# Attention with shifted queries: the sum of queries and maxima moved from a PSUM bank to GpSimd

## Chip, cores and metric

One core of one Trainium2 chip. The metric is the device time of one execution in microseconds (us); lower is better. The kernel was executed three times for timing and once more with the hardware profiler.

## What is computed

A hidden state of 16 x 256 tokens with 128 features goes through a transformer layer with experts, then through a retention block, then through the same layer again. The attention of such a layer, for one batch element and head, is this:

```
xn = layer_norm(x)                       # 256 tokens x 128
q, k, v = xn @ Wq + bq, xn @ Wk + bk, xn @ Wv + bv
for each of 16 heads (8 features each):
    s = q_h @ k_h.T / sqrt(8)            # 256 x 256
    p = exp(s - max(s, keys))            # the shift cancels below
    out_h = (p @ v_h) / sum(p, keys)
x1 = layer_norm(x + out @ Wo + bo) * g1 + b1
```

Behind it each token goes to one of four expert networks by a router, and a second layer norm follows.

## The kernel before

The layer runs as two phases (`phase(0)` and `phase(BATCH)`), each over 16 batch elements, with the retention block between them and the experts' tiles at the end of each. Elements are numbered 0 to 15 in the first phase and 16 to 31 in the second. The engines are driven by five instruction streams written out by hand; each engine works its stream strictly in order and waits on semaphores. For every element `i` a function `body(i)` per engine holds the work of iteration `i`, and this work is software-pipelined: iteration `i` also does parts of elements `i + 2` (layer norm before attention, "prep"), `i + 1` (projection), `i - 1` (the rest of its heads), `i - 2` (output projection, layer norm "ln1", x1), `i - 3` (router positions) and `i - 4` (sorted rows written to memory, `sort_out`).

An iteration has eight slots, p = 0 to 7. In slot p, TensorE issues a burst (`score_burst`): the raw scores of heads 2p and 2p + 1 of element i (L591), interleaved with the shifted, transposed scores (L597) of two heads that are five slots behind. VectorE takes the negated maximum over the raw scores (`maximum`, L1374), which lie in one pair of PSUM banks (`score_duo`); ScalarE takes the exponential of the shifted scores (`exp`, L1064) from another pair (`prob_duo`). Neither pair is doubled, so the next burst waits for both.

Heads are handled in four groups g of four. The stacked queries `q_st` and keys `k_st` of a group are made by `expand` (L584, L585) on TensorE and `out_expand` (L1050) on ScalarE. Once all the maxima of group g are there, they have to be added to the queries: in the stack, each head has spare rows beside its 8 feature rows, and one of them carries the shift, so that the product of stacks gives score minus maximum. This is `spread_max`, L629 and L631: TensorE first copies the queries `q_st[:, g]` through an identity into a spare bank (256 columns), then adds the transposed maxima from `mx` (two matmuls of 128 columns). ScalarE's `shift_q` (L1056) copies the sum to `q2_st[:, g]` in SBUF, rounded to fp32r, and signals `q2_ready`. It runs in slot 3 for g = 0, slot 5 for g = 1, slot 7 for g = 2 and slot 1 of the next iteration for g = 3. Its reader, the L597 part of the burst, comes two slots later each time: slots 5, 7, and 1 and 3 of the next iteration. The spare bank `a` (or `c`) is taken by `take`, which waits for the last reader of the bank; in slot 2 `expand` for g = 2 takes bank `a` after `shift_q` for g = 3 of the element before.

GpSimd's stream in iteration i is: place the first half of the values (`place_v(i, 0)`, L1867), the two indirect DMAs of `sort_out(i - 4)` (L1907), the layer norm "prep" for i + 2 (`rstd`, L1842 to L1846, `normalise`, L1854), `add_bo` (L1859), the layer norm "ln1" for i - 2 (L1842 to L1846, L1854), `make_x1` (L1872, L1874), `route_product` (L1880), `own_row` (L1892), and the second half of the values (`place_v(i, 1)`, L1867). The values come from one buffer `v_nat`, which ScalarE fills (`out_v`, L1043) in slot 1: it waits until both halves of the element before have been placed (`vb_ready`). In slot 1 ScalarE's order is `exp`, `out_v`, `out_pv` (L1072), `shift_q` for g = 3; all its later work stands behind them.

The calls in GpSimd's `body(i)` that the change goes between are

```
if live(i, base):
    place_v(i, 0)
...
    add_bo(i + 2, base)
...
    normalise(i - 2, "ln1", lambda t: y1[:, t, :], lambda t: n1[:, t, :], i - 1 - base // BATCH)
    make_x1(i - 2, base)
```

## Time and profile before

| | us |
|---|---|
| median of three timed runs | 901.46 (901.03 to 902.38) |
| profiled execution, its own time | 902.45 |
| its span in the trace | 900.6 |
| TensorE matmul / weight load busy | 812.1 / 609.2 |
| VectorE busy | 740.8 |
| ScalarE busy | 650.5 |
| GpSimd busy | 549.7 |

The profiled execution took 902.45 us, 1.85 us more than its span, which begins with the first instruction shown and ends with the last. Engines are named PE (TensorE matmuls), PEld (TensorE weight loads), DVE (VectorE), ACT (ScalarE), POOL (GpSimd) and SP (SyncE). Busy times overlap. A line such as L1374 is a line of the kernel. Ends of matmuls are modelled, and they are pipelined, so matmuls that stand in a row overlap in the trace. In a timeline, `[0.21 <-POOL v_st L1867]` means that the engine idled 0.21 us before the instruction and that the one named released it; a line with xN merges N instructions, and starts of neighbours on one engine can overlap by the pipeline of the engine.

### The profile page before, as it was taken

What the parts mean: (1) busy time and instruction counts of PE and PEld (TensorE: products, weight loads), DVE (VectorE), ACT (ScalarE), POOL (GpSimd) and SP (SyncE); (2) the same over time, 40 slices, a digit from 0 to 9 for tenths busy, and PEclk for the clock granted to TensorE, in tenths of its full rate; (3) what the DMA queues carried; (4) which work ended last, traced back from release to release, by engine and by line L of the source; (5) the groups of instructions that cost most, each with busy time, mean ns of one, the idle gap of its engine ahead of it and who ended that gap; (6) DMA issues with size and microseconds to landing.
All of it is one profiled execution on the core that took longest, in us unless ns stands there. A gap on an engine that the chain in (4) does not pass through costs nothing.

```text
span 900.6 us, 26130 instructions
## 1 busy us (share of the span) xinstructions
PE 812.1 (90%) x8479; PEld 609.2 (68%) x8479; DVE 740.8 (82%) x1841; ACT 650.5 (72%) x1242; POOL 549.7 (61%) x914
## 2 busy tenths in 40 slices
PE   4989999999999699399999988999999999987894
PEld 3656666666665699367878766666666666656894
DVE  4688999999996788569898875789998989967895
ACT  2578888888886488335454554888989889873794
POOL 4126667676755667628676772157676766556676
PEclk9999999999999999789999996999999999999997
DMA  9995699100004688210000000000000000045781
GB/s 281 378 419 143 126 401 415 70 12 24 12 18 145 194 235 275 74 46 2 0 0 0 1 1 1 2 2 14 24 12 23 12 18 18 14 150 171 235 276 49
DMA packets 41813, 96.65 MB, mean 107 GB/s; under 512 B 5224, under 2 KB 25470, under 8 KB 37260
## 3 DMA queue, kind: packets, MB, share of 16 engines
q1 hardware_dynamic: 36236, 83.11, 28.3%
q0 software_dynamic: 5504, 12.63, 3.9%
q8 instruction: 37, 0.61, 0.3%
q14 instruction: 36, 0.29, 0.1%
HBM read 43.64 MB, written 53.13 MB: 107 GB/s over the span
## 4 chain that ended last, share of the span: by engine, by line
PE 57%; DVE 16%; POOL 11%; issue 11%; ACT 2%; DMA 2%; DVEq 0%; SPq 0%; POOLq 0%; ACTq 0%
PE duo L648 10%; PE duo L591 10%; DVE mx L1374 6%; PE duo L584 4%; PE duo L740 3%; PE duo L900 2%; PE duo L585 2%; PE duo L629 2%; PE duo L879 2%; PE duo L567 2%; PE duo L888 2%; PE duo L858 2%; POOL out L1964 2%; PE duo L861 2%; PE duo L631 2%
## 5 line engine op out<-in xcount | busy, mean ns | idle before, releaser
L1374 DVE TENSOR_REDUCE mx<-duo 128x4 fp32r<-128x1024 f32 x256 | 313.5, 1225 | 64.5 <-PE duo L591 57.5
L1064 ACT ACTIVATE probs<-duo 128x1024 f32<-128x1024 f32 x256 | 262.8, 1027 | 42.1 <-PE duo L597 33.8
L591 PE MATMUL duo<-stacks 32*128 32x256 f32 x1024 | 133.4, 339 | 24.7 <-DVE mx L1374 19.9
L648 PE MATMUL duo<-probs,v_st 128*32 128x256 f32 x2048 | 143.1, 399 | 0.5
L597 PE MATMUL duo<-q_st,stacks 32*128 32x256 f32 x1024 | 131.6, 335 | 0.1
L591 PEld LDWEIGHTS duo<-stacks 32*128 32x128 f32 x1024 | 80.3, 191 | 69.0 <-DVE mx L1374 27.0
L1050 ACT ACTIVATE stacks<-duo,small 128x512 fp32r<-128x512 f32 x128 | 88.8, 694 | 9.0 <-PE duo L585 8.4
L584 PE MATMUL duo<-qk_hi,sel_r 128*128 128x256 f32 x256 | 82.5, 342 | 4.1 <-DVE qk_lo L1363 3.5
L648 PEld LDWEIGHTS duo<-probs,v_st 128*32 128x32 f32 x2048 | 54.8, 112 | 42.8 <-issue 4.8
L740 PE MATMUL duo<-w,xs 128*128 x608 | 78.1, 283 | 5.9 <-DVE hidden L1542 2.8
L740 PEld LDWEIGHTS duo<-w,xs 128*128 128x128 f32 x608 | 73.8, 198 | 7.9 <-issue 7.7
L597 PEld LDWEIGHTS duo<-q_st,stacks 32*128 32x128 f32 x1024 | 78.2, 188 | 1.4 <-ACT probs L1064 0.5
L1907 POOL DMA_INDIRECT x_sorted<-rows,pos_all x64 | 66.9, 1045 | 13.0 <-issue 13.0
L1056 ACT ACTIVATE q_st<-duo 128x256 fp32r<-128x256 f32 x128 | 49.4, 386 | 34.5 <-PE duo L631 33.4
L585 PE MATMUL duo<-qk_lo,sel_r 128*128 128x256 f32 x256 | 69.2, 291 | 0.0
L1842 POOL TENSOR_TENSOR a_prep<-mv_prep,eps_ln 128x2 f32<-128x2 f32 x32 | 6.0, 189 | 102.2 <-DVE mv_prep L1339 102.2
L1094 ACT ACTIVATE xs<-duo,wside 128x256 f32<-128x256 f32 x152 | 59.2, 470 | 9.1 <-PE duo L726 8.8
L584 PEld LDWEIGHTS duo<-qk_hi,sel_r 128*128 128x128 f32 x256 | 50.4, 197 | 21.0 <-ACT q_st L1056 5.1
L1867 POOL TENSOR_TENSOR v_st<-v_nat,ones_wide 128x128 f32<-128x128 f32 x64 | 29.6, 462 | 49.1 <-ACT v_nat L1043 28.9
L1679 DVE TENSOR_TENSOR ret<-duo,dm 128x768 f32<-128x768 f32 x64 | 58.0, 947 | 1.2 <-PE duo L882 1.2
L629 PE MATMUL duo<-stacks,ident_r 128*128 128x256 f32 x128 | 53.0, 414 | 0.0
L629 PEld LDWEIGHTS duo<-stacks,ident_r 128*128 128x128 f32 x128 | 24.6, 193 | 41.6 <-issue 36.9
(222 smaller groups left out, 2057.7 us busy)
## 6 DMA issues: line engine op xcount, KB each, us to landing
x_sorted<-ret SPq DMA_DIRECT2D x2, 17476.0 KB, 52.7
wbuf<-w_pack SPq DMA_DIRECT2D x38, 512.0 KB
ret<-x_sorted SPq DMA_DIRECT2D x22, 257.0 KB, 3.1
stacks<-x_sorted SPq DMA_DIRECT2D x12, 257.0 KB, 3.9
wside<-w_pack SPq DMA_DIRECT2D x38, 66.0 KB
w_pack<-wbuf SPq DMA_DIRECT2D x2, 1024.0 KB, 8.4
decay_rows<-prow SPq DMA_DIRECT2D x1, 1536.0 KB
xs<-x_sorted SPq DMA_DIRECT2D x4, 257.0 KB, 3.6
```

Source lines behind the costliest of these rows:

```text
L584: pe.matmul(half, sel_r[:, g, 2 * n, :], qk_hi[:, n, :], start=True, stop=False)
L585: last = pe.matmul(half, sel_r[:, g, 2 * n + 1, :], qk_lo[:, n, :], start=False, stop=True)
L591: return pe.matmul(score_bank[h % 2][:, t * SEQ:(t + 1) * SEQ], q_st[r:r + 32, g, t * P:(t + 1) * P], k_st[r:r + 32, g, :], start=True, st ...
L597: return pe.matmul(banks[h % 2][:, t * SEQ:(t + 1) * SEQ], k_st[r:r + 32, g, t * P:(t + 1) * P], q2_st[r:r + 32, g, :], start=True, stop=True)
L629: pe.matmul(o[:, 0:SEQ], ident_r[:], q_st[:, g, :], start=True, stop=True)
L648: last = pe.matmul(into[32 * j:32 * j + 32, :], v_st[:, half, t, first:first + VC], probs[:, (g * GH + j) % RING, t, :], start=(t == 0 and ...
L740: last = pe.matmul(sum_bank(k)[:, t * P:(t + 1) * P], hid[:, n % 2, c, t * P:(t + 1) * P], w2[:, bass.ds(e * CPE + c, 1), :], start=(c == ...
L1050: act.activation(both_st[:, :, g, :], o.rearrange("p (n t) -> p n t", n=2), ACT.Identity, bias=ones_col[:]).then_inc(ex_ready, 1)
L1064: act.activation(probs[:, h % RING:h % RING + 2, :, :], duo_now[:].rearrange("p (n t q) -> p n t q", n=2, t=TT), ACT.Exp, scale=SCALE).the ...
L1094: act.activation(hid[:, n % 2, c, :], bank[c][:, 0:SEQ], ACT.Relu, bias=wside[:, n % 3, c:c + 1]).then_inc(h_ready, 1)
L1374: dve.tensor_reduce(rows, score_duo[:].rearrange("p (n t k) -> p n t k", n=2, t=TT), AX.X, ALU.max, negate=True).then_inc(max_done, 1)
L1907: pool.indirect_dma_start(x_sorted[b // BATCH], bass.IndirectOffsetOnAxis(pos_all[:, b - base, t:t + 1], 0), rows[:, b - base, t, :], None ...
```

## The change

The matmul that copied the queries into the bank is gone, so the bank holds the transposed maxima alone. `shift_q` copies them to a new SBUF buffer `shift_rows`, two groups deep, and signals `shift_ready`, which now also frees the bank. A new function `add_shift` on GpSimd adds `q_st` and `shift_rows` into `q2_st` and signals `q2_ready`. It stands at four places of GpSimd's stream. (Element i - 2 exists from the third iteration of a phase; before that `add_shift(i, 2)` follows `add_shift(i, 1)` directly.)

```diff
+        shift_rows = sb("shift_rows", [P, 2, SEQ])
...
             def spread_max(b, g):
                 pe.wait_ge(max_done, b * PAIRS + 2 * g + 2)
-                o = take("aaca"[g], q2_ready, b * 4 + g + 1)
-                pe.matmul(o[:, 0:SEQ], ident_r[:], q_st[:, g, :], start=True, stop=True)
+                o = take("aaca"[g], shift_ready, b * 4 + g + 1)
                 for t in range(TT):
-                    last = pe.matmul(o[:, t * P:(t + 1) * P], mx[:, g % 2, t, :], ident_r[:], start=False, stop=True, skip_group_check=True)
+                    last = pe.matmul(o[:, t * P:(t + 1) * P], mx[:, g % 2, t, :], ident_r[:], start=True, stop=True)
                 last.then_inc(m_ps, 1)
...
-                        turn["a"], turn["c"] = (q2_ready, (i - 1) * 4 + 2), (q2_ready, (i - 1) * 4 + 3)
+                        turn["a"], turn["c"] = (shift_ready, (i - 1) * 4 + 2), (shift_ready, (i - 1) * 4 + 3)
...
             def shift_q(b, g):
                 act.wait_ge(m_ps, b * 4 + g + 1)
-                wait(act, prob_ps, (b - 1) * (NH // 2) + 2 * g + 2)
-                act.activation(q2_st[:, g, :], (bank_a, bank_a, bank_c, bank_a)[g][:, 0:SEQ], ACT.Copy).then_inc(q2_ready, 1)
+                wait(act, q2_ready, b * 4 + g - 1)
+                act.activation(shift_rows[:, g % 2, :], (bank_a, bank_a, bank_c, bank_a)[g][:, 0:SEQ], ACT.Copy).then_inc(shift_ready, 1)
...
+            def add_shift(b, g):
+                pool.wait_ge(shift_ready, b * 4 + g + 1)
+                wait(pool, prob_ps, (b - 1) * (NH // 2) + 2 * g + 2)
+                pool.tensor_tensor(q2_st[:, g, :], q_st[:, g, :].bitcast(FP32), shift_rows[:, g % 2, :], ALU.add).then_inc(q2_ready, 1)
...
                     if live(i, base):
                         place_v(i, 0)
+                    if live(i - 1, base):
+                        add_shift(i - 1, 3)
                     if live(i, base) and live(i - 4, base):
                         sort_out(i - 4, base, (i - 1) * (NH // 2) + 6)
+                    if live(i, base):
+                        add_shift(i, 0)
...
                         add_bo(i + 2, base)
+                    if live(i, base):
+                        add_shift(i, 1)
+                    if live(i, base) and not live(i - 2, base):
+                        add_shift(i, 2)
...
                         normalise(i - 2, "ln1", lambda t: y1[:, t, :], lambda t: n1[:, t, :], i - 1 - base // BATCH)
+                        if live(i, base):
+                            add_shift(i, 2)
                         make_x1(i - 2, base)
```

GpSimd's stream in a steady iteration before, from the residual row of the layer norm "prep" to the issues of the sorted rows (a_ln, c_ln and rstd_ln belong to the layer norm "ln1"):

```order
L1859 TENSOR_TENSOR rows<-s_nat,vecs_sb 128x2x128 [waits prep_ln]
L1842 TENSOR_TENSOR a_ln<-mv_ln,eps_ln 128x2 [waits ln1]
L1844 TENSOR_TENSOR c_ln<-mv_ln,minus_one 128x2
L1846 TENSOR_TENSOR rstd_ln<-a_ln,half_root 128x2 [waits ln1]
L1854 TENSOR_SCALAR token_bufs<-token_bufs,c_ln,rstd_ln 128x128 [waits neg_mean_ln1,ln1,x1_ready]
L1854 TENSOR_SCALAR token_bufs<-token_bufs,c_ln,rstd_ln 128x128
L1872 TENSOR_TENSOR token_bufs<-token_bufs,vecs_sb 128x256 [waits ln1]
L1874 TENSOR_TENSOR rows<-token_bufs,vecs_sb 128x2x128 [waits x1_ready]
L1880 TENSOR_TENSOR token_bufs<-rows,vecs_sb 128x256 [waits router,x1_ready]
L1892 TENSOR_TENSOR rows<-xs,vecs_sb 128x2x128 [waits y1_ready]
L1867 TENSOR_TENSOR v_st<-v_nat,ones_wide 128x4x4x8 [waits pv_done]
L1867 TENSOR_TENSOR v_st<-v_nat,ones_wide 128x4x4x8 [waits pv_done,v_ready]
```

The same stretch of the changed kernel (its line numbers are one higher in front of the new function and seven higher behind it):

```order
L1866 TENSOR_TENSOR rows<-s_nat,vecs_sb 128x2x128 [waits prep_ln]
L1861 TENSOR_TENSOR q_st<-stacks,shift_rows 128x256 [waits prob_ps,shift_ready]
L1843 TENSOR_TENSOR a_ln<-mv_ln,eps_ln 128x2 [waits ln1]
...
L1855 TENSOR_SCALAR token_bufs<-token_bufs,c_ln,rstd_ln 128x128
L1861 TENSOR_TENSOR q_st<-stacks,shift_rows 128x256 [waits prob_ps,shift_ready]
L1879 TENSOR_TENSOR token_bufs<-token_bufs,vecs_sb 128x256 [waits ln1]
...
L1874 TENSOR_TENSOR v_st<-v_nat,ones_wide 128x4x4x8 [waits pv_done,v_ready]
L1861 TENSOR_TENSOR q_st<-stacks,shift_rows 128x256 [waits prob_ps,shift_ready]
L1894 TENSOR_TENSOR tick<-ones_wide 1x1 [waits pos_ready,row_ready,x1_ready]
```

The adds (L1861; the program calls `q2_st` by its neighbour's name, q_st) stand, in this order, for g = 1 behind `add_bo`, for g = 2 between `normalise` and `make_x1`, and for g = 3 of the element before in front of `sort_out`. The one for g = 0 stands behind the DMA issues of `sort_out`.

TensorE in slot 1 before (values weighed, maxima spread for g = 3, then slot 2's burst):

```order
L648 MATMUL duo<-probs,v_st 32x256 x7
L629 MATMUL duo<-stacks,ident_r 128x256 [waits ex_ready,max_done]
L631 MATMUL duo<-ident_r,mx 128x128 x2
L591 MATMUL duo<-stacks 128x256 [waits exp_done,max_done,ex_ready]
```

In the changed kernel the first of the two transposes takes over the waits:

```order
L632 MATMUL duo<-ident_r,mx 128x128 [waits ex_ready,max_done]
L632 MATMUL duo<-ident_r,mx 128x128
```

## Rows read from the trace of the kernel before

**Rows 1.** The page: busy time of each engine, and the chain by engine.

```profile
PE 812.1 (90%) x8479; PEld 609.2 (68%) x8479; DVE 740.8 (82%) x1841; ACT 650.5 (72%) x1242; POOL 549.7 (61%) x914
...
PE 57%; DVE 16%; POOL 11%; issue 11%; ACT 2%; DMA 2%; DVEq 0%; SPq 0%; POOLq 0%; ACTq 0%
```

**Rows 2.** Groups: line, engine, shapes, count | busy us, mean ns | idle before.

```profile
L1374 DVE TENSOR_REDUCE mx<-duo 128x4 fp32r<-128x1024 f32 x256 | 313.5, 1225 | 64.5 <-PE duo L591 57.5 <-issue 0.2
L629 PE MATMUL duo<-stacks,ident_r 128*128 128x256 f32 x128 | 53.0, 414 | 0.0
L1872 POOL TENSOR_TENSOR token_bufs<-token_bufs,vecs_sb 128x256 f32<-128x256 f32 x30 | 22.0, 735 | 2.5
L1880 POOL TENSOR_TENSOR token_bufs<-rows,vecs_sb 128x256 f32<-128x256 f32 x30 | 20.5, 685 | 2.3
L2007 POOL TENSOR_TENSOR qk<-att_un 128x512 f32<-128x512 f32 x16 | 20.5, 1278 | 39.3 <-DVE att_un L1692 39.3
```

**Rows 3.** Timeline of VectorE: start us, us; first maxima of four elements, one of slot 3.

```profile
560.44 1.23 DVE L1374 TENSOR_REDUCE mx<-duo 128x4 fp32r<-128x1024 f32 x1 [2.20 <-PE duo L591]
...
577.83 1.23 DVE L1374 TENSOR_REDUCE mx<-duo 128x4 fp32r<-128x1024 f32 x1
...
593.10 1.23 DVE L1374 TENSOR_REDUCE mx<-duo 128x4 fp32r<-128x1024 f32 x1
...
608.94 1.23 DVE L1374 TENSOR_REDUCE mx<-duo 128x4 fp32r<-128x1024 f32 x1
...
725.35 1.23 DVE L1374 TENSOR_REDUCE mx<-duo 128x4 fp32r<-128x1024 f32 x1 [0.18 <-PE duo L591]
```

**Rows 4.** Windows: us, busy of each engine, clock share, DMA share, GB/s.

```profile
560.00:578.00 18.00, 17.32 (x180) 11.62 (x177) 11.88 (x17) 14.14 (x24) 3.48 (x8) 0.84 0.01 1
...
593.00:609.00 16.00, 15.61 (x186) 10.77 (x183) 14.39 (x33) 14.04 (x25) 8.52 (x18) 1.00 0.00 2
```

**Rows 5.** Timeline of POOL in one steady element, slot 6 to slot 5.

```profile
715.50 0.73 POOL L1859 TENSOR_TENSOR rows<-s_nat,vecs_sb 128x256 f32<-128x256 f32 x1
717.01 0.19 POOL L1842 TENSOR_TENSOR a_ln<-mv_ln,eps_ln 128x2 f32<-128x2 f32 x1 [0.79 <-DVE mv_ln L1339]
...
719.14 0.73 POOL L1872 TENSOR_TENSOR token_bufs<-token_bufs,vecs_sb 128x256 f32<-128x256 f32 x1
...
722.14 0.46 POOL L1867 TENSOR_TENSOR v_st<-v_nat,ones_wide 128x128 f32<-128x128 f32 x1
723.16 0.46 POOL L1867 TENSOR_TENSOR v_st<-v_nat,ones_wide 128x128 f32<-128x128 f32 x1 [0.55 <-ACT v_nat L1043]
...
725.79 0.98 POOL L1907 DMA_INDIRECT x_sorted<-rows,pos_all  x1 [0.16 <-issue]
729.07 0.18 POOL L1842 TENSOR_TENSOR a_prep<-mv_prep,eps_ln 128x2 f32<-128x2 f32 x1 [2.30 <-DVE mv_prep L1339]
```

**Rows 6.** Timeline of ACT: first gated v_nat of phase two, and the same steady element.

```profile
596.49 0.38 ACT L1043 ACTIVATE v_nat<-duo 128x256 f32<-128x256 f32 x1 [0.50 <-POOL v_st L1867]
...
718.90 0.38 ACT L1056 ACTIVATE q_st<-duo 128x256 fp32r<-128x256 f32 x1 [0.42 <-PE duo L631]
...
722.70 0.38 ACT L1043 ACTIVATE v_nat<-duo 128x256 f32<-128x256 f32 x1 [0.21 <-POOL v_st L1867]
...
723.24 0.39 ACT L1056 ACTIVATE q_st<-duo 128x256 fp32r<-128x256 f32 x1
```

**Rows 7.** Timeline of PE: slot 7's burst and spread, expand in slot 2, slot 3's burst.

```profile
716.87 0.39 PE L591 MATMUL duo<-stacks 32*128 32x256 f32 x2
...
718.31 0.39 PE L629 MATMUL duo<-stacks,ident_r 128*128 128x256 f32 x1
718.53 0.33 PE L631 MATMUL duo<-ident_r,mx 128*128 128x128 f32 x2
...
723.69 0.39 PE L584 MATMUL duo<-qk_hi,sel_r 128*128 128x256 f32 x1
...
724.80 0.38 PE L591 MATMUL duo<-stacks 32*128 32x256 f32 x2
```

More of the change, by code:

```diff
@@ L340, in build @@
         prob_ps, exp_done, pv_done = sem("prob_ps"), sem("exp_done"), sem("pv_done")
+        shift_ready = sem("shift_ready")
         un_ready, att_ps, att_ready = sem("un_ready"), sem("att_ps"), sem("att_ready")
```

## Prediction

> **What bounds the kernel now.** I read the page first: its busy shares and its chain of work that ended last [rows 1]. TensorE is busy 90% of the span and holds 57% of the chain, so a matmul removed looks like a gain. But the same chain gives POOL (GpSimd) 11%, though POOL is busy only 61%: somewhere everyone waits for GpSimd, and that is the engine that gets the new work.
>
> The grouped instructions give the prices [rows 2]. The copy of the queries is 128 matmuls of 414 ns on average (L629), and GpSimd's additions of 128x256 cost 685 to 735 ns (L1880, L1872). VectorE's maximum (L1374) is 256 times 1225 ns. Each burst of score matmuls waits for the maximum of the last burst, since both use the one pair of score banks, and the maximum waits for the burst: the **score loop**. Eight bursts make one batch element.
>
> How long an element takes is read from VectorE's timeline at the first maximum of elements 18, 19 and 20 [rows 3]: 593.10 - 577.83 = 15.27 us, then 608.94 - 593.10 = 15.84 us. What is new in the second is, among other things, the path through GpSimd. The windows show TensorE busy 15.61 of 16 us there, at full clock, 1.00, that is 2.4 GHz [rows 4].
>
> Then one steady element in the timelines, engine by engine. GpSimd [rows 5]: it ends the residual row (L1859, 715.50 + 0.73 = 716.23), starts the layer norm at 717.01 once VectorE has the moments, and from 719.14 works without a gap, x1 twice, router product, own row, until the second half of the values is placed: 722.14 + 0.46 = 722.60. ScalarE [rows 6] starts the next element's v_nat at 722.70, 0.10 us later and after 0.21 us of idling for just that. Its next two instructions, the last one L1056 at 723.24, follow at once. TensorE [rows 7] starts expand (L584) at 723.69, 0.06 us after L1056 has ended at 723.63, and the burst of slot 3 at 724.80. So **the path through GpSimd ends last in slots 0 to 3**: own row, values placed, v_nat, shifted queries, expand, burst. It has no slack that I can find.
>
> **The change part by part.** The order of instructions shows that every element gets four adds on GpSimd (g = 0 to 3), each behind a wait on shift_ready, and that TensorE loses L629 before each pair of L631.
>
> *TensorE, L629 removed.* In slot 7 it starts at 718.31 and the first L631 at 718.53 [rows 7]: 0.22 us per group, 128 x 0.22 = 28 us of TensorE's time. It is worth that only where TensorE orders the next burst. In a steady element the score loop comes to the same time: the burst at 724.80 gives the maximum at 725.35 [rows 3], 1.23 us, and the next burst could not start before 726.58 and a semaphore's way. I count the gain only in the two first elements of each phase, where the GpSimd path is loose: 4 elements x 4 x 0.22 = 3.5 us, of which I take 2. Elsewhere it only brings ScalarE's copy 0.22 us forward.
>
> *The add for g = 1*, behind add_bo (L1859). add_bo ends at 716.23; with 0.04 to start, 0.73 for the add (as L1872) and 0.10 for the way to TensorE (as from v_st to v_nat, 722.60 to 722.70) it is there at 717.10; slot 7's burst, which reads it, starts at 716.87 today [rows 7]. The burst is 0.23 us later. Behind it waits the layer norm, which starts at 717.01 today and would start at 717.05: covered.
>
> *The add for g = 2*, between normalise and make_x1. It waits for ScalarE's copy of slot 7, today 718.90 + 0.38 = 719.28 [rows 6]; 0.22 earlier for L629, 0.23 later for the burst: 719.29. Then 0.08 to GpSimd (as from 723.08, the end of v_nat, to 723.16 [rows 5]), 0.73, and 0.07: make_x1 starts at 720.17 instead of 719.14. **That is 1.03 us**, 0.80 for the add and 0.23 of waiting for ScalarE's copy, and all that stands behind it moves with it: values placed, v_nat, the copy for g = 3, expand, and by that the burst of slot 3. Slot 1's burst, which reads this add, comes at 720.80 today; the add ends at 720.10: covered by 0.6 us.
>
> *The add for g = 3*, behind place_v(i, 0). Its copy ends at 723.63 + 1.03 = 724.66, the add at 724.66 + 0.08 + 0.73 = 725.47, with the way 725.57; slot 3's burst starts at 724.80 + 1.03 = 725.83. Covered by 0.26. Queued behind it are sort_out's two indirect DMA issues, on this same queue. The last ends today at 725.79 + 0.98 = 726.77; placed values and add put them some 1.03 + 0.8 later, 728.6.
>
> *The add for g = 0*, behind sort_out: 728.6 + 0.8 = 729.4. Today POOL idles 2.30 us before a_prep at 729.07 [rows 5], which itself will be at 730.1. It fits, cover 0.7. Slot 5's burst, its reader, would be at about 729.9: 0.4 to spare. This add costs nothing.
>
> *ScalarE* has the same copy with another target, no price. Its new wait is for the add two groups back, long done. The new buffer is SBUF, no DMA is added.
>
> **Price of an add.** The trace has no GpSimd add with a rounded (fp32r) output and two full SBUF operands of 256 columns. From below: 0.69 us (L1880). From above: 1.28 us (L2007, two full operands, but 512 columns wide [rows 2]). I take 0.73, the row with the same width. VectorE writes fp32r in this trace (L1374, 1225 ns for 1024 columns) at no surcharge that would show.
> The Trainium skill (GPSIMD Engine Reference, section 3.1) puts a two-input tensor_tensor at about 2.6 cycles per element at 1.2 GHz, and section 4.1 says to keep elementwise adds on VectorE. By the rate alone the add would be an estimated 0.55 us without its dispatch, and the sum below some 9 us smaller (two adds on the path, 26 elements); the measured rows decide. The rule itself speaks against this change.
>
> **The sum.** The gate (place_v of one element, v_nat of the next) is closed by GpSimd where make_x1 runs in the body and another element follows: 13 times in a phase, in the second phase for the first time at 596.49 (idle 0.50 us for it) [rows 6], 26 in all. Some of the 1.03 can be lost where TensorE or the exponentials would have held slot 3 a little anyway; I take 1.00. 26 x 1.00 = +26 us; -2 us for the first elements. From the profiled execution's 902.45 us: 926.5. The three timed runs have their median at 901.46, 1.0 lower, so 925.5 against them; I write 926. An element would take 15.8 + 1.0 = 16.8 us.
>
> **The rivals.**
> *Heavier.* If the add takes 1.00 us instead of 0.73, g = 1 and g = 2 each bring 0.27 more and g = 3 just uses up its cover: 1.6 us an element, 26 x 1.6 = 42 us, 943. Also TensorE's clock may fall: it will be busy about 14.7 of 16.8 us, 0.88, while the window 560 to 578 shows 17.32 of 18 busy at a mean clock of 0.84, so some of it at 1.2 GHz [rows 4]; so a busy engine can still be at the lower level. The Trainium skill (TensorE: Matmul & The Clock Gate, part 1) says the gate follows how busy the engine has lately been; that rule would point to this rival. The element in the 0.84 window took 17.39 us (577.83 - 560.44, [rows 3]) against 15.27, 2.1 more; if four elements were hit, +8. Together 935 to 950. Chance 0.22.
> *Faster: the adds are hidden and the score loop sets the pace.* POOL has 39% of idle time, and if the layer norm's work had slack, the bursts would go at the pace of element 18. Price: 15.84 - 15.27 = 0.57 us x 26 = 15 us, and 2 more: 885. It decides at one place: the values must be placed no later than 722.60. For it: POOL's idle gaps before 717.01 and 729.07. Against: none of these gaps lies between 717.01 and 722.60, and one add stands there. Chance 0.05.
> *No change:* the 1.03 is absorbed in slots 0 to 3 because ScalarE's and TensorE's queues close up behind v_nat. Against: expand follows L1056 by 0.06 us today. 26 x 0 and -2: 900. Chance 0.04.
> *The change does not do what it says:* the order shows L629 gone and the adds in; no chance given.
>
> **How the numbers follow.** The forecast has 0.69: 926, and its own range 912 (26 x 0.69 for a bare add, less 4) to 936. The range reaches up to most of the heavier case and takes in the lower bound: 908 to 950. A difference under 0.2% (1.8 us) is about what a measurement of this kernel can't tell from none. Faster 0.05, same 0.04, slower 0.91.
>
> **What would show it.** Right: elements of about 16.8 us; v_nat's idle time for v_st up from 0.2 to over 1 us each, POOL's share of the chain up; L629's place in the chain gone without effect; adds of 0.7 us; DVE waiting longer for the slot 3 burst. Wrong: v_nat starting 0.1 us after exp with no idle time; elements at 15.3 us; adds over 1 us; or the lost time in slots 5 to 7 in place of slots 2 and 3.

## The result, and the profile after

The changed kernel takes **942.55 us** (median of four runs, 938.91 to 948.96), the kernel before 901.25 us (897.20 to 902.38): a ratio of **1.050** (95% interval 1.045 to 1.054). Executions that came out over 1.5% above the fastest of the same kernel are left out of every median and ratio in this document. The forecast was 926, with a range of 908 to 950. The direction and the mechanism in the running phases were right, the size was short by 16.5 us. The profiled execution took 941.01 us; its span is 939.2, against 900.6 before, 38.6 more.

The page of the changed kernel, busy times and chain:

```profile
PE 817.5 (87%) x8351; PEld 602.3 (64%) x8351; DVE 755.7 (80%) x1841; ACT 648.0 (69%) x1242; POOL 641.2 (68%) x1042
...
PE 44%; POOL 19%; issue 12%; DVE 10%; ACT 2%; DMA 1%; POOLq 0%; ACTq 0%; DVEq 0%
```

TensorE lost 128 matmuls (8479 to 8351) and 13 points of the chain; GpSimd gained 128 adds, 91.5 us of busy time, and went from 11% of the chain to 19% [rows 1]. It is still busy only 68% of the span.

The group of the adds (columns as in [rows 2]) and two rows of the waits (waiter <- releaser: idle us in all, count, the longest):

```profile
L1861 POOL TENSOR_TENSOR q_st<-stacks,shift_rows 128x256 fp32r<-128x256 f32 x128 | 94.0, 735 | 80.6 <-ACT shift_rows L1057 75.8 <-PE duo L599 1.0
```

```profile
ACT v_nat L1044 <- POOL v_st L1874: 23.6, 24, 1.3
...
PE duo L599 <- POOL q_st L1861: 8.0, 4, 3.8
```

An add costs 735 ns, as forecast. v_nat waits for the placed values 24 times, 23.6 us in all, 0.98 us each, where it idled 0.21 us in the steady element of before [rows 6]. (In the kernel before only 10 of the 32 v_nat wait for them, 2.9 us in all, and only two of these in the first phase: the element of [rows 6] is one of the later ones in this.) The second row was not forecast: the score matmuls wait for an add four times, twice for 3.8 us, once at the end of each phase; the two others are under 0.2 us.

VectorE's timeline at the first maximum of elements 18 to 21 of the changed kernel:

```profile
598.84 1.23 DVE L1375 TENSOR_REDUCE mx<-duo 128x4 fp32r<-128x1024 f32 x1
...
614.07 1.23 DVE L1375 TENSOR_REDUCE mx<-duo 128x4 fp32r<-128x1024 f32 x1
...
630.87 1.23 DVE L1375 TENSOR_REDUCE mx<-duo 128x4 fp32r<-128x1024 f32 x1
...
647.53 1.23 DVE L1375 TENSOR_REDUCE mx<-duo 128x4 fp32r<-128x1024 f32 x1
```

Element 18, where GpSimd's path is still loose, takes 15.23 us (before 15.27 [rows 3]); the next two take 16.80 and 16.66. Over both phases a steady element takes 16.70 us where it took 15.8: **+0.9 us** (forecast +1.0).

Where in the element? Slot j is here the time from maximum j to maximum j + 1 of an element, in us, each the mean of ten elements of a phase, first phase / second phase:

| slot | 0 | 1 | 2 | 3 | 4 | 5 | 6 | 7 |
|---|---|---|---|---|---|---|---|---|
| before | 1.89 / 1.90 | 1.96 / 1.96 | 2.03 / 2.00 | 1.99 / 1.98 | 2.02 / 2.02 | 2.01 / 2.03 | 1.87 / 1.86 | 2.10 / 2.02 |
| after | 1.90 / 1.89 | 1.90 / 1.97 | **2.77 / 2.81** | 1.98 / 1.98 | 2.02 / 2.02 | 1.95 / 1.95 | **2.06 / 2.05** | 2.10 / 2.00 |

Two slots grew: slot 2, which ends with the maximum of slot 3's burst (+0.74 and +0.81), and slot 6, which ends with that of slot 7's burst (+0.19). These are the two places that the forecast priced. Slots 1 and 5 are up to 0.08 us shorter; b_nocopy below shows the same of the missing copy. In one steady element they look so. GpSimd:

```profile
712.83 0.88 POOL L1855 TENSOR_SCALAR token_bufs<-token_bufs,c_ln,rstd_ln 128x128 f32<-128x128 f32 x2 [0.17 <-POOL rstd_ln L1847]
714.11 0.74 POOL L1861 TENSOR_TENSOR q_st<-stacks,shift_rows 128x256 fp32r<-128x256 f32 x1 [0.40 <-ACT shift_rows L1057]
714.80 0.73 POOL L1879 TENSOR_TENSOR token_bufs<-token_bufs,vecs_sb 128x256 f32<-128x256 f32 x1
...
717.80 0.46 POOL L1874 TENSOR_TENSOR v_st<-v_nat,ones_wide 128x128 f32<-128x128 f32 x1
718.81 0.46 POOL L1874 TENSOR_TENSOR v_st<-v_nat,ones_wide 128x128 f32<-128x128 f32 x1 [0.55 <-ACT v_nat L1044]
719.36 0.73 POOL L1861 TENSOR_TENSOR q_st<-stacks,shift_rows 128x256 fp32r<-128x256 f32 x1
```

ScalarE, then TensorE:

```profile
718.35 0.38 ACT L1044 ACTIVATE v_nat<-duo 128x256 f32<-128x256 f32 x1 [1.03 <-POOL v_st L1874]
...
718.89 0.39 ACT L1057 ACTIVATE shift_rows<-duo 128x256 f32<-128x256 f32 x1
```

```profile
719.34 0.39 PE L586 MATMUL duo<-qk_hi,sel_r 128*128 128x256 f32 x1
...
720.45 0.38 PE L593 MATMUL duo<-stacks 32*128 32x256 f32 x2
```

Normalise ends at 713.71; the add for g = 2 waits 0.40 us for its copy, and make_x1 starts at 714.80, 1.09 us after normalise. Nothing but the work of before follows until the values are placed, 717.80 + 0.46 = 718.26; v_nat starts 0.09 later, after idling 1.03; L1057 ends at 719.28 and expand starts 0.06 later; slot 3's burst comes at 720.45. The add for g = 3 ends at 720.09 and is ready for it.

**Where the 38.6 us are.** Five stretches of the span, bounded by the first maximum of the phase's first and last element, by ScalarE's first experts' tile behind it (L1094 / L1095), and by the first maximum of the second phase:

| stretch | before | after | more |
|---|---|---|---|
| 15 elements, phase 1 | 248.4 | 259.8 | +11.4 |
| last element's first maximum to the experts, phase 1 | 25.6 | 32.9 | **+7.4** |
| experts and retention | 249.9 | 251.8 | +1.9 |
| 15 elements, phase 2 | 244.5 | 256.1 | +11.7 |
| last element's first maximum to the experts, phase 2 | 25.8 | 31.5 | **+5.7** |
| the rest | 106.5 | 107.1 | +0.6 |

The elements cost 23.1 us, against a forecast of +26 and -2. The two ends of the phases cost 13.1 us, which the forecast has not at all. An end has two parts, divided by the last maximum of the phase. Behind that maximum it takes 15.1 / 14.5 us where it took 9.7 / 9.8: **+5.4 and +4.7**. The bursts of the last element before it take 17.8 / 17.1 where they took 15.8 / 16.0, +2.0 and +1.1; this part also varies between kernels that have no add in it (see a_drain).

GpSimd at the end of phase 1, changed kernel:

```profile
297.70 0.46 POOL L1874 TENSOR_TENSOR v_st<-v_nat,ones_wide 128x128 f32<-128x128 f32 x1
...
298.46 1.10 POOL L1914 DMA_INDIRECT x_sorted<-rows,pos_all  x1 [0.17 <-issue]
299.87 0.96 POOL L1914 DMA_INDIRECT x_sorted<-rows,pos_all  x1 [0.30 <-issue]
300.85 0.73 POOL L1861 TENSOR_TENSOR q_st<-stacks,shift_rows 128x256 fp32r<-128x256 f32 x1
```

TensorE waits for that add, and ScalarE had ended the copy that it needs at 297.19:

```profile
301.64 0.81 PE L599 MATMUL duo<-q_st,stacks 32*128 32x256 f32 x8 [3.81 <-POOL q_st L1861]
```

```profile
296.80 0.39 ACT L1057 ACTIVATE shift_rows<-duo 128x256 f32<-128x256 f32 x1
```

The add for g = 3 of the last element belongs to the next iteration of GpSimd's stream, so it stands behind everything of the last one: x1, product, own row, values, and two DMA issues of `sort_out`, which stand at the end of a phase's last iteration (`sort_out(i - 3)`). In a running phase the next element's bursts fill that time; here there is no next element, and nothing hides it. The same row stands at the end of phase 2, with 3.80 us.

### The profile page after: what moved, and what is told of

Its sections match the earlier page's. It is cut to its first block, busy times and chain, and to the rows that moved or that the text cites. A ratio compares the mean times of both kernels' runs of the same rounds, so it can differ in the third digit from the quotient of the medians.

```text
span 939.2 us, 26128 instructions
## 1 busy us (share of the span) xinstructions
PE 817.5 (87%) x8351; PEld 602.3 (64%) x8351; DVE 755.7 (80%) x1841; ACT 648.0 (69%) x1242; POOL 641.2 (68%) x1042
## 4 chain that ended last, share of the span: by engine, by line
PE 44%; POOL 19%; issue 12%; DVE 10%; ACT 2%; DMA 1%; POOLq 0%; ACTq 0%; DVEq 0%
PE duo L649 10%; PE duo L593 7%; DVE mx L1375 5%; PE duo L586 4%; POOL out L1981 3%; POOL x_mid L1981 3%; PE duo L901 2%; PE duo L632 2%; POOL q_st L1861 2%; PE duo L587 2%; PE duo L880 2%; ACT shift_rows L1057 2%; POOL rows L1881 2%; POOL xs L1972 2%; POOL token_bufs L1879 2%
## 5 line engine op out<-in xcount | busy, mean ns | idle before, releaser
L1375 DVE TENSOR_REDUCE mx<-duo 128x4 fp32r<-128x1024 f32 x256 | 313.4, 1224 | 77.4 <-PE duo L593 73.3
L593 PE MATMUL duo<-stacks 32*128 32x256 f32 x1024 | 135.9, 342 | 33.1 <-DVE mx L1375 23.6
L1861 POOL TENSOR_TENSOR q_st<-stacks,shift_rows 128x256 fp32r<-128x256 f32 x128 | 94.0, 735 | 80.6 <-ACT shift_rows L1057 75.8
L649 PE MATMUL duo<-probs,v_st 128*32 128x256 f32 x2048 | 147.7, 409 | 0.0
L593 PEld LDWEIGHTS duo<-stacks 32*128 32x128 f32 x1024 | 83.8, 195 | 82.1 <-DVE mx L1375 31.9
L632 PEld LDWEIGHTS duo<-ident_r,mx 128*128 128x128 f32 x256 | 42.4, 197 | 43.3 <-issue 36.7
L1057 ACT ACTIVATE shift_rows<-duo 128x256 f32<-128x256 f32 x128 | 49.4, 386 | 27.7 <-PE duo L632 27.7
L1095 ACT ACTIVATE xs<-duo,wside 128x256 f32<-128x256 f32 x152 | 59.5, 470 | 9.5 <-PE duo L727 9.2
L632 PE MATMUL duo<-ident_r,mx 128*128 128x128 f32 x256 | 60.8, 320 | 0.0
L587 PEld LDWEIGHTS duo<-qk_lo,sel_r 128*128 128x128 f32 x256 | 51.8, 202 | 0.0
```

The costliest lines, as they stand in the source:

```text
L587: last = pe.matmul(half, sel_r[:, g, 2 * n + 1, :], qk_lo[:, n, :], start=False, stop=True)
L593: return pe.matmul(score_bank[h % 2][:, t * SEQ:(t + 1) * SEQ], q_st[r:r + 32, g, t * P:(t + 1) * P], k_st[r:r + 32, g, :], start=True, st ...
L632: last = pe.matmul(o[:, t * P:(t + 1) * P], mx[:, g % 2, t, :], ident_r[:], start=True, stop=True)
L649: last = pe.matmul(into[32 * j:32 * j + 32, :], v_st[:, half, t, first:first + VC], probs[:, (g * GH + j) % RING, t, :], start=(t == 0 and ...
L1057: act.activation(shift_rows[:, g % 2, :], (bank_a, bank_a, bank_c, bank_a)[g][:, 0:SEQ], ACT.Copy).then_inc(shift_ready, 1)
L1375: dve.tensor_reduce(rows, score_duo[:].rearrange("p (n t k) -> p n t k", n=2, t=TT), AX.X, ALU.max, negate=True).then_inc(max_done, 1)
```

## Experiments

Twelve runs were made, in four groups, each group with the kernel before on its own chip. That kernel's median moved between 897.1 and 901.3 us over the chips, and single executions of it spread over 891 to 907. The lengths of steady elements in the traces of the changed kernel and of its repetition agree to 0.1 us, so I read both; their ends do not agree so well (31.5 and 32.9 us in phase 2). "End" is the stretch from the last element's first maximum to the experts' first tile, phase 1 / phase 2 (before 25.6 / 25.8; after 32.9 / 31.5).

| run | ratio to before (95%) | median | steady element | slot 2 | end |
|---|---|---|---|---|---|
| b_nocopy | 0.993 (0.989 to 0.997) | 896.7 | 15.7 | 2.00 / 2.11 | 25.5 / 25.9 |
| b_add2 | 1.018 (1.013 to 1.024) | 915.9 | 16.33 | 2.53 / 2.57 | 24.2 / 25.0 |
| a_early | 1.011 (1.007 to 1.015) | 908.8 | 15.8 | 1.89 / 1.88 | 31.0 / 30.4 |
| b_early | 0.998 (0.994 to 1.001) | 898.0 | 15.86 | 2.06 / 2.05 | 24.2 / 25.5 |
| a_drain | 1.034 (1.027 to 1.042) | 929.1 | 16.7 | 2.77 / 2.80 | 28.0 / 27.2 |
| a_add1 | 1.041 (1.032 to 1.049) | 935.4 | 16.45 | 2.77 / 2.80 | 32.0 / 31.5 |
| a_all | 0.999 (0.995 to 1.003) | 898.5 | 15.57 / 15.48 | 1.91 / 1.90 | 28.0 / 28.2 |
| b_early_nocopy | 0.999 (0.995 to 1.003) | 898.8 | 15.80 / 15.74 | 2.09 / 2.10 | 25.7 / 25.5 |
| a_best | **0.994 (0.990 to 0.997)** | 895.9 | 15.58 / 15.48 | 1.91 / 1.90 | 25.9 / 26.1 |
| a_again | 1.037 (1.030 to 1.044) | 938.0 | 16.7 | 2.77 / 2.81 | 32.4 / 32.9 |
| b_early_spare | 0.997 (0.994 to 1.001) | 894.5 | 15.72 / 15.66 | 1.89 / 1.89 | 27.3 / 24.6 |
| b_early_nocopy_spare | 0.995 (0.992 to 0.998) | 893.0 | 15.58 / 15.52 | 1.89 / 1.90 | 25.7 / 25.8 |

### The two halves of the change alone

**b_nocopy**, the kernel before without the copy of the queries; the maxima alone go into the shifted queries.

```diff
-                pe.matmul(o[:, 0:SEQ], ident_r[:], q_st[:, g, :], start=True, stop=True)
...
-                    last = pe.matmul(o[:, t * P:(t + 1) * P], mx[:, g % 2, t, :], ident_r[:], start=False, stop=True, skip_group_check=True)
+                    last = pe.matmul(o[:, t * P:(t + 1) * P], mx[:, g % 2, t, :], ident_r[:], start=True, stop=True)
```

> The kernel before without the matmul that copies the queries into the bank (L629); the shifted queries then hold the maxima alone, so the attention is wrong in value, and the time is that of TensorE's relief alone. Theory (the path through GpSimd and the score loop set the pace, the copy's 28 us are hidden): elements stay at 15.7 to 15.9 us, time 897 to 902. Rival (TensorE orders the bursts, the copy counted in full): 0.22 us x 4 per element, elements at 14.9 us, time 875 to 885.

Measured: 0.1 us per element, 0.993 (0.989 to 0.997). The removed matmuls held 53.0 us of TensorE's busy time [rows 2] and 128 x 0.22 = 28 us of its pace. By the elements, 0.1 us in each of some 30, they give back about 3 us; the ratio would make it 6, with an interval from 2 to 10. The gain lies in slots 1, 5 and 6, each 0.02 to 0.06 us shorter, and not in slot 2 (2.00 / 2.11 for 2.03 / 2.00).

**b_add2**, the kernel before with a sum that nobody reads, at the place of the add for g = 2. It waits for nothing.

```diff
+            def spare_add():
+                pool.tensor_tensor(spare_sum[:], spare[:, 0, :], spare[:, 1, :], ALU.add)
...
+                        if live(i, base):
+                            spare_add()
                         make_x1(i - 2, base)
```

> The kernel before with one additional GpSimd add of 128x256 that nobody waits for, between the layer norm and x1 (where the change has its add for g = 2). Theory (that stretch of GpSimd's stream has no slack in 26 elements): each add costs its 0.73 us and the way to the next, elements at 16.5 us, time 901 + 26 x 0.75 = 920 (916 to 923). Rival (only the waits for the adds' results cost, a queue place costs nothing): 901 to 903.

Measured: elements +0.52, all of it in slot 2, and no end of a phase is longer. ScalarE's timeline of this run:

```profile
716.19 0.38 ACT L1045 ACTIVATE v_nat<-duo 128x256 f32<-128x256 f32 x1 [0.67 <-POOL v_st L1873]
```

So 0.7 us in GpSimd's queue there costs 0.5 us per element, though nothing reads the result. It is 0.2 short of the price of an add: the path had a slack of about 0.2 us on average.

### Is it the placed values?

**a_early** places the second half of the values ahead of the add for g = 2, with all four adds kept. **b_early** does the same to the kernel before.

```diff
                         normalise(i - 2, "ln1", lambda t: y1[:, t, :], lambda t: n1[:, t, :], i - 1 - base // BATCH)
+                        if live(i, base):
+                            place_v(i, 1)
...
-                    if live(i, base):
+                    if live(i, base) and not live(i - 2, base):
                         place_v(i, 1)
```

> The changed kernel with the second half of the values placed right behind the layer norm ln1, ahead of the add for g = 2, x1, router product and own row. Theory (the change costs what it does by way of place_v and v_nat): v_nat no longer waits for GpSimd, slot 2 falls from 2.80 back to about 2.0 us, elements at 15.7 to 16.1 us, time 942 - 26 x 0.75 = 922 (915 to 926), since what the end of the phases lost stays. Rival (the waits of the bursts for the adds themselves set the pace): elements stay over 16.5 us, time over 935.

> The kernel before with the second half of the values placed right behind the layer norm ln1. Theory (the path through GpSimd ends last in slots 0 to 3 of 26 elements; the score loop stands just below it): elements from 15.8 to 15.4 or 15.5 us, time 890 to 896. Rival (TensorE and the score loop are as late as GpSimd, so nothing is won): 900 to 903.

a_early: elements back to 15.8, slot 2 to 1.89, 908.8 us. Its ScalarE no longer idles for the values, while its GpSimd works almost without a gap from 719.0 to 730.0:

```profile
724.58 0.38 ACT L1044 ACTIVATE v_nat<-duo 128x256 f32<-128x256 f32 x1
```

```profile
721.03 0.46 POOL L1874 TENSOR_TENSOR v_st<-v_nat,ones_wide 128x128 f32<-128x128 f32 x1
721.47 0.73 POOL L1861 TENSOR_TENSOR q_st<-stacks,shift_rows 128x256 fp32r<-128x256 f32 x1
...
725.59 0.74 POOL L1861 TENSOR_TENSOR q_st<-stacks,shift_rows 128x256 fp32r<-128x256 f32 x1
```

That shows it: the adds as such cost nothing in slot 2, their place ahead of the values did. It came out better than expected (909 for 922). Of the 31.6 us by which its span is shorter than that of the changed kernel, 25.4 lie in the fourth to the fifteenth element of the two phases, where 26 x 0.75 = 19.5 was expected, and 3.1 in the ends. The other 3 lie in the first three elements of phase 2, which ran at a mean granted clock of 0.81, for 0.70 in the changed kernel's trace, and have nothing to do with the edit as far as I can see. Nearly all of what is left over the kernel before lies in the ends, 31.0 and 30.4.

b_early missed its expectation: v_nat no longer waits, and the element stays as long as it was. Taking GpSimd out of the loop is worth nothing to the kernel before. Something else is just as late.

### The ends of the phases, and slot 6

**a_drain** moves the add for g = 3 of a phase's last element only, to a place before the last two steps of that iteration.

```diff
-                    if live(i - 1, base):
+                    if live(i - 1, base) and not is_last(i - 1, base):
                         add_shift(i - 1, 3)
...
                         route_product(i - 2, base)
+                        if is_last(i, base):
+                            add_shift(i, 3)
```

> The changed kernel with one add in another place: the add for g = 3 of the last element of a phase stands between its router product and own row instead of behind the two DMA issues of sort_out. Theory (12 to 13 us of the loss lie behind the last element of each phase, where TensorE waits for this add): elements stay at 16.7 us, the way from the last element's first maximum to the first ReLU falls from 32.9 and 31.5 us to 27 to 29, time 942 - 8 = 934 (930 to 938). Rival (the drain is longer for another reason, such as the clock or the tables): 32 us and 942 as before.

Measured: the ends go from 32.9 / 31.5 to 28.0 / 27.2, 9.2 us for two adds moved, and the steady element stays at 16.7. Nearly all of it, 4.9 and 4.2, lies behind the last maximum of the phase. The idle time of 3.81 us is now

```profile
297.79 0.77 PE L599 MATMUL duo<-q_st,stacks 32*128 32x256 f32 x8 [0.21 <-POOL q_st L1861]
```

4.9 us in phase 1 is more than 3.81 - 0.21 = 3.6. The windows over the end of phase 1 (columns as in [rows 4]) show where the rest is. The changed kernel:

```profile
274.50:283.00 8.50, 4.37 (x52) 2.96 (x53) 8.26 (x18) 5.46 (x10) 6.54 (x13) 0.99 0.04 15
283.00:290.00 7.00, 6.98 (x58) 3.72 (x62) 3.75 (x11) 3.15 (x5) 0.55 (x1) 0.52 0.33 87
290.00:297.30 7.30, 6.27 (x75) 3.70 (x76) 4.48 (x12) 5.88 (x10) 5.67 (x11) 1.00 0.92 292
297.30:300.30 3.00, 0.54 (x4) 0.34 (x4) 2.57 (x12) 0.96 (x1) 2.52 (x5) 0.93 0.32 107
300.30:307.40 7.10, 5.76 (x47) 2.67 (x48) 0.42 (x1) 2.71 (x5) 5.97 (x11) 0.55 0.09 30
```

And a_drain:

```profile
283.00:290.00 7.00, 7.00 (x62) 3.63 (x62) 3.59 (x11) 3.40 (x5) 0.40 (x1) 0.55 0.35 90
290.00:302.30 12.30, 10.68 (x123) 6.48 (x120) 8.21 (x24) 9.21 (x15) 10.23 (x19) 1.00 0.64 210
```

Behind the stall the changed kernel runs 7.10 us at a mean granted clock of 0.55, nearly all of it at 1.2 GHz, after TensorE was busy for 0.54 of 3.00 us. Without the stall the clock stays at 2.4 GHz to the end. So the stall is paid twice, as idle time and in the pace of what follows. Another such stretch, 283 to 290, is in both, behind one in which TensorE was busy 4.37 of 8.50 us. The kernel before has a milder one there (next fence: its two rows), behind 4.61 of 6.00 us busy; that is part of the 2.4 us by which a_drain's end is still longer than 25.6, of which 1.9 lie in the last element's bursts.

```profile
264.00:270.00 6.00, 4.61 (x54) 3.18 (x54) 5.75 (x16) 4.47 (x9) 4.09 (x9) 1.00 0.06 22
...
273.50:280.00 6.50, 5.88 (x72) 3.16 (x68) 3.98 (x10) 3.75 (x5) 1.16 (x4) 0.82 0.59 170
```

Whether this stretch comes does not depend on the adds. The row of the last element's bursts of phase 1 in b_add2, and the one in b_early_spare, neither of which has an add that anyone waits for:

```profile
278.00:284.00 6.00, 5.38 (x79) 3.34 (x79) 4.96 (x18) 4.38 (x6) 0.36 (x3) 1.00 0.34 74
```

```profile
270.00:279.00 9.00, 8.38 (x87) 4.49 (x83) 5.19 (x18) 4.72 (x7) 0.59 (x3) 0.67 0.49 138
```

At 1.00 these bursts take 14.5 us, at 0.67 they take 17.6. So of the 13.1 us of the ends, the 10.0 behind the last maximum belong to the change, 9.1 of them to the two adds that a_drain moves. Of the 3.1 in the last element's bursts, 1.3 lie in its first three slots (7.2 us in both phases, for 6.5 and 6.7), ahead of this stretch; they are there in a_drain too, and I have not traced them. The other 1.8 cannot be told from the scatter.

**a_add1** moves the add for g = 1 one step forward.

```diff
+                        if live(i, base):
+                            add_shift(i, 1)
                         add_bo(i + 2, base)
-                    if live(i, base):
+                    if live(i, base) and not live(i + 2, base):
                         add_shift(i, 1)
```

> The changed kernel with the add for g = 1 ahead of add_bo instead of behind it. Theory (this add's late result costs 0.2 us of slot 6 and, through the later copy for g = 2, as much in the path to v_nat): slot 6 falls from 2.06 to 1.87 us, elements from 16.7 to 16.5 us, time 942 - 26 x 0.2 = 937. Rival (the path is set by the adds' durations alone): slot 6 falls, slot 2 rises by as much, elements stay at 16.7.

Measured: slot 6 goes from 2.06 to 1.83, the element from 16.70 to 16.45, and slot 2 does not move. The term of 0.23 us that the forecast gave to g = 1 is 0.25.

**a_all** has the three moves together (a_early, a_drain, a_add1).

> The changed kernel with all three moves: values placed behind the layer norm, the add for g = 1 ahead of add_bo, the last element's add for g = 3 ahead of own row. Theory (each add can have a place where nobody waits for it): elements at 15.6 to 15.7 us, way to the first ReLU 25.5 to 27 us, time 895 to 900, at or a little below the kernel before. Rival (GpSimd as a whole is now too busy): elements at 16 us or more, over 905.

Elements as expected, 15.57 and 15.48, below those of the kernel before; the ends stayed at 28, where 25.5 to 27 was expected. Behind the last maximum they take 10.6 / 10.7 us, 0.9 each more than in the kernel before: each of the last adds still stands between a copy and a burst that has nothing else to wait for (TensorE idles 0.44 and 0.21 us for them). The other 1.6 and 1.5 us lie in the last element's bursts. The time is that of the kernel before, 0.999 (0.995 to 1.003): the elements' gain pays for the ends.

### What holds the kernel before at 15.8 us?

**b_early_nocopy**: both reliefs at once, GpSimd's (b_early) and TensorE's (b_nocopy).

> The kernel before without the copying matmul (attention wrong in value, since the shifted queries hold the maxima alone) and with the values placed early, so that both TensorE and GpSimd are relieved. Theory (two paths of the same length stand side by side in slots 0 to 3, so each relief alone gives nothing): elements at 15.4 to 15.6 us, time 888 to 894. Rival (a third limit, the exponentials or the maxima, stands at the same height): elements at 15.7 us as with the relief of TensorE alone, time 895 to 898.

A miss: 15.80 and 15.74, and slot 2 even longer, 2.09. With GpSimd and TensorE both relieved there had to be another path. I looked for it in VectorE. VectorE and GpSimd in b_early, slot 2:

```profile
710.12 0.38 DVE L1426 CAST rint<-rkey 128x2 int32<-128x2 f32 x1
...
711.02 1.23 DVE L1374 TENSOR_REDUCE mx<-duo 128x4 fp32r<-128x1024 f32 x1
```

```profile
709.43 1.10 POOL L1907 DMA_INDIRECT x_sorted<-rows,pos_all  x1 [0.17 <-issue]
```

A cast of two numbers per partition takes 0.38 us, and ends at 710.50, 1.07 us into GpSimd's issue of an indirect DMA. VectorE has no idle time between it and the maximum of slot 3's burst. In the kernel before, b_early, b_nocopy and b_early_nocopy nearly all of these casts take either 0.15 to 0.19 us or 0.37 to 0.46, by when they start. The group of it in b_early, and in b_nocopy:

```profile
L1426 DVE CAST rint<-rkey 128x2 int32<-128x2 f32 x32 | 11.2, 349 | 0.1
```

```profile
L1425 DVE CAST rint<-rkey 128x2 int32<-128x2 f32 x32 | 6.7, 208 | 0.1
```

**b_early_spare** and **b_early_nocopy_spare** test that by adding work: one unread sum on GpSimd right ahead of `sort_out`, so that the issue starts 0.7 us later and the cast falls into its first part or before it.

```diff
+                        spare_add()
                         sort_out(i - 4, base, (i - 1) * (NH // 2) + 6)
```

> The kernel before with values placed early (the run with elements at 15.85 us) and one more GpSimd add of 128x256 that nobody waits for, right ahead of the DMA issues of sort_out. Theory (with values placed early, VectorE's cast in slot 2 falls into the last part of a 1.1 us DMA issue on GpSimd and is held until 1.07 us of it have gone, 0.25 us longer; that and not a third limit eats the relief): the cast is back at 0.16 us, slot 2 falls from 2.05 to 1.9 us, elements to 15.65 or 15.7 us, so more work on GpSimd makes the attention shorter by 26 x 0.17 = 4 us: 894 to 899. Rival (ScalarE's exponentials or TensorE set slot 2): cast short, slot 2 at 2.05, elements at 15.85 us or above.

> The same add in the kernel that also lacks the copying matmul (attention wrong in value, since the shifted queries hold the maxima alone). Theory: slot 2 from 2.09 to 1.9 us, elements from 15.77 to 15.5 us, as in the kernel with all three moves; time 889 to 895. Rival: elements stay at 15.77 us.

Group of the cast and the DMA issue after the added sum, b_early_spare:

```profile
L1428 DVE CAST rint<-rkey 128x2 int32<-128x2 f32 x32 | 6.6, 207 | 0.1
```

```profile
703.08 0.74 POOL L1860 TENSOR_TENSOR spare_sum<-spare 128x256 fp32r<-128x256 f32 x1
...
704.27 1.11 POOL L1913 DMA_INDIRECT x_sorted<-rows,pos_all  x1 [0.17 <-issue]
```

With one *more* sum per element slot 2 falls from 2.06 to 1.89 and from 2.10 to 1.90, and the elements from 15.86 to 15.7 and from 15.77 to 15.55. So two paths ended within about 0.2 us of each other in slot 2 of the kernel before: GpSimd's values, and VectorE's cast behind a DMA issue, which was only just in time there and was held as soon as the values came early. TensorE's copy of the queries is not a third one in that slot: with both others loosened slot 2 is 1.89 us with the copy and 1.89 / 1.90 without it. Its 0.14 us per element lie in slots 1, 5 and 6. In time, b_early_spare cannot be told from before (0.997, 0.994 to 1.001); with all three gone it is 0.995 (0.992 to 0.998), in a kernel that leaves the copy out.

### A version that beats both

**a_best** has the early values, the add for g = 1 ahead of `add_bo`, and the sum on GpSimd wherever elements follow each other. For groups 2 and 3 of a phase's last element it goes back to the matmul and ScalarE's copy straight into `q2_st`, for which TensorE then waits (not shown).

```diff
+                whole = is_last(b, base) and g >= 2
+                if whole:
+                    pe.matmul(o[:, 0:SEQ], ident_r[:], q_st[:, g, :], start=True, stop=True)
...
+                if g >= 2 and (is_last(b, 0) or is_last(b, BATCH)):
...
+                    act.activation(q2_st[:, g, :], (bank_a, bank_a, bank_c, bank_a)[g][:, 0:SEQ], ACT.Copy).then_inc(shift_ready, 1)
```

> As the kernel with values placed early and the add for g = 1 ahead of add_bo, and for groups 2 and 3 of the last element of a phase the sum is made as before the change (TensorE copies the queries into the bank, ScalarE writes the sum). Theory (in the drained stretch each hop over GpSimd is in sight, since nothing else stands between the copy and its reader): elements stay at 15.5 us, way to the first ReLU back from 28 to 25 or 26 us, time 5 us less than with all three moves, 892 to 897, under the kernel before. Rival (the stretch's 28 us come from the clock, whatever the adds do): 28 us and 899.

**a_again** is the changed kernel once more, on the same chip.

> The changed kernel itself once more, on the chip of the run beside it. The times of the kernel before have scattered by 1% between runs; expected here: a ratio of 1.04 to 1.05 to the kernel before, elements at 16.7 us, way to the first ReLU 31 to 33 us.

a_best: ends 25.9 and 26.1, elements 15.58 and 15.48, and 0.994 (0.990 to 0.997) of the kernel before, 895.9 for 899.9 us. It computes all that the reference does. Of the 2.1 us by which each of its ends is shorter than in a_all, 0.9 and 0.8 lie behind the last maximum, where no add is left to wait for. The other 1.2 and 1.3 lie in the last element's bursts, which no edit touches; there the granted clock of phase 1 was 0.88 in the slowest stretch (269.5 to 275), for 0.65 in a_all (271 to 277). So the rival that named the clock is right for more than half of it. a_again took 938.0, ratio 1.037 (1.030 to 1.044), with elements of 16.7 and ends of 32.4 / 32.9. Between its two measurements the changed kernel's cost is 38 to 41 us, and the intervals of the two ratios (1.045 to 1.054 the first time) do not meet: between two groups of runs a ratio can move by 1%. That a_best is ahead of the kernel before rests therefore on its shorter elements (15.58 for 15.87 and 15.48 for 15.77) as much as on the 0.6% in time.

## Why the prediction was right or wrong

**The path** (own row, values placed, v_nat, shifted queries, expand, burst): right for the changed kernel, and shown by a_early, where moving the values alone takes the element from 16.7 to 15.8 with every add in place. "It has no slack that I can find" was a little off: b_add2 puts 0.7 us into it and gets 0.5. The one element that was read is of those in which v_nat waits; in 22 of 32 it did not wait in the kernel before.

**Price of an add**, 0.73: 0.735. The fp32r output has no surcharge. The rate of the Trainium skill (GPSIMD Engine Reference, section 3.1) had made an estimated 0.55 without dispatch; the row is 0.18 above that.

**g = 2**, 1.03 us: make_x1 starts 1.09 us behind normalise's end, of it 0.40 waiting for the copy. v_nat's waits were forecast at over 1 us each and are 0.98. **g = 1**, 0.23: 0.25 by a_add1. **g = 3 and g = 0** covered in a steady element: slots 3, 4, 5 and 7 did not grow. **Element**, 16.8: 16.7. **26 elements**, +26 - 2 = +24: measured +23.1, but in part by luck. v_nat waits in 24 elements and not in 26; in the last element of a phase slot 2 is as long as before (2.18 and 2.17 us). In the 24 the loss is 0.96 us each, also since the last but one element of a phase grows by 1.3 (17.7 for 16.4, 0.5 of it in slot 7). The first three elements of the phases bring nothing in sum, where -2 stood.

**The copy's removal**, counted at 2 us in the first elements: b_nocopy gets about 3 us, spread over all elements. In the main that was right: of the 28 us of TensorE's time nearly all is off the path.

**The step that failed is the sum itself**: it stops at the elements. "26 x 1.00 = +26 us; -2 us for the first elements" took every place where one element follows another and nothing behind the last one. For g = 3 the prediction named `sort_out`'s DMA issues as *queued behind* the add. For a phase's last element the order is the other way round, the add stands behind those issues, and the time in which the next element's bursts cover it does not exist. The ends grew by 7.4 + 5.7 = 13.1 us, 10.0 of it behind the last maximum, where this add stands. a_drain takes 9.2 us away with two moved adds, and in a_best the ends are almost those of before (25.9 and 26.1 against 25.6 and 25.8; behind the last maximum 9.8 and 9.9 against 9.7 and 9.8). The order of instructions showed this before any run: the iteration behind the last has the add and no work ahead of it that could hide it. Another 1.9 us between the phases and 0.6 outside them I have not traced.

**The range.** 908 to 950 held the result only because it reached up into the heavier case; the forecast's "own range", 912 to 936, did not hold it. Its lower end is also added up wrongly: 26 x 0.69 less 4 on top of 902 is about 916.

**Heavier rival.** Its time, 943, is the one measured, by luck and for reasons that are in the main not its own. The add did not take 1.00 us. The clock in the steady stretch did not fall:

```profile
647.00:664.00 17.00, 15.49 (x184) 10.32 (x184) 15.07 (x33) 14.12 (x24) 13.66 (x26) 1.00 0.04 15
```

TensorE is busy 15.49 of 17 us there, 0.91 (0.88 was forecast), and stays at 2.4 GHz. One element of phase 1 is an exception: it took 18.1 us, in a window with a mean granted clock of 0.91. In the last element's bursts and at the drained end the clock fell to 0.52 and 0.55, each time after TensorE had idled (the windows under a_drain). The rule of the Trainium skill that the prediction named (TensorE: Matmul & The Clock Gate, part 1), that the gate follows how busy the engine has lately been, agrees with these rows; what was wrong was where I looked for the idle time.

**Faster rival**, 885 by the pace of element 18. Its condition, values placed in time, was met by b_early, and the kernel took 898.0, not 885. The condition was not sufficient: VectorE's held cast took the place of the values in slot 2. Even with all three reliefs the element takes 15.5 and not 15.27.

**No change**, 900: excluded; nothing closes up behind v_nat.

## What to carry to other kernels

When work moves to an engine that works in order, price it by what stands behind it in the queue up to the next hand-over, not by the engine's idle share: the same four adds, with the copy gone, make an element 0.9 us longer in one order and 0.3 us shorter in another. Then walk through the last iteration by itself, since a cover that consists of the next element's work is missing there, and the stall can pull the clock down with it. And before you pay for relieving one path, look how late the next one is, in more than one element; here GpSimd's could go without a gain.

## What the hardware showed that I had not expected

**VectorE is held by GpSimd's DMA issue, but only in its last part.** In the kernel before and in b_early, b_nocopy and b_early_nocopy, `sort_out`'s first indirect DMA issue lasts 1.10 us. A cast of 128x2 on VectorE that starts up to 0.56 us into it takes 0.15 to 0.19 us, and so does one that starts at 1.05 or later. One that starts at 0.61 to 0.70 us ends at 1.06 to 1.08 us, in all 44 cases, and takes 0.37 to 0.46. (Two casts in each kernel lie behind the end of a phase, in an issue of 1.12 or 1.19 us on which a GpSimd sum follows at once; they take 0.73 us although one of them starts 0.54 us into it, and I leave them open.) The kernel before has four such held casts, all in its first phase, and four elements there of 15.98 to 16.00 us, where their neighbours take 15.8. In the changed kernel the same small VectorE instructions end with a GpSimd sum. VectorE:

```profile
717.76 0.52 DVE L1425 TENSOR_SCALAR rkey<-rkey,vecs_sb 128x2 f32<-128x2 f32 x1
...
719.51 0.60 DVE L1429 TENSOR_TENSOR rint<-rint,rkey 128x2 int32<-128x2 int32 x1
```

They end at 718.28 and 720.11; GpSimd's placing of the values ended at 718.26 and its add for g = 3 at 720.09. The maxima, which read PSUM, never grew: 1224 ns on average after, 1225 before [rows 2]. The Trainium skill (SBUF — State Buffer, section "Who interferes with whom") has VectorE and GpSimd share one pair of ports as an exclusive lock, held for a whole instruction; for the sums these rows agree, for the DMA issue the trace shows a hold of the last part only.

**A sum more made a kernel's elements shorter** (15.86 to 15.7 us in b_early_spare), for this reason and no other that I found: it moved the issue out from under the cast.
